# Layer 0's attention in a fused two-layer kernel: first routing in three bursts, first rows on ScalarE, later statistics and routing behind the attention

## The reference

```python
x = x + tanh(g_xattn[0]) * L0_xattn(layernorm(x), ctx, ctx)   # 16 heads of 8 channels, softmax
x = x + tanh(g_ffn[0])   * L0_ffn(layernorm(x))               # 8 experts, the best 2 per token
x = x + tanh(g_xattn[1]) * L1_xattn(layernorm(x), ctx, ctx)   # one head, causal
x = x + tanh(g_ffn[1])   * L1_ffn(layernorm(x))               # 8 experts, each takes its best 17 tokens
```

## Time and profile before

| what | value |
|---|---|
| median of three timed runs | 1021.94 us (1019.55 to 1022.29) |
| profiled execution, span from first to last instruction | 1023.1 us |
| TensorE busy | 910.3 us (89%) |
| VectorE busy | 599.0 us (59%) |
| ScalarE busy | 554.5 us (54%) |
| GpSimd busy | 647.5 us (63%) |
| mean granted TensorE clock | 0.971 of 2.4 GHz |

### The profile page before, as it was taken

The page is one execution under the profiler, slowest core; times in us unless marked ns, Lnnn a source line. Parts: engine busy times, 40 slices in busy tenths (PEclk is TensorE's granted clock), DMA queues, the critical chain, the costliest instruction groups (busy, mean ns, idle before and its releaser), DMA issues.

```text
span 1023.1 us, 24907 instructions
## 1 busy us (share of the span) xinstructions
PE 910.3 (89%) x8860; PEld 761.7 (74%) x8860; DVE 599.0 (59%) x1580; ACT 554.5 (54%) x1313; POOL 647.5 (63%) x807
## 2 busy tenths in 40 slices
PE   5998999888439999899999999968998999999992
PEld 3776777667328989799989988865776766778881
DVE  6887889999527463245625769984635324433320
ACT  2787877776224545344544766635555455444440
POOL 6353455468754777677427777721886658878885
PEclk9999999999859999999999999999999999999997
DMA  9364433112525656666566663141354635575453
GB/s 372 119 205 159 144 138 131 36 48 75 179 81 166 215 166 218 199 195 190 162 182 194 194 238 104 54 112 42 67 74 46 123 37 54 95 93 54 50 57 44
DMA packets 130154, 130.73 MB, mean 128 GB/s; under 512 B 32882, under 2 KB 102770, under 8 KB 129138
## 3 DMA queue, kind: packets, MB, share of 16 engines
q1 hardware_dynamic: 99810, 91.69, 28.5%
q0 software_dynamic: 28928, 29.91, 18.1%
q10 hardware_dynamic: 1296, 7.54, 1.8%
HBM read 53.88 MB, written 49.62 MB: 101 GB/s over the span
## 4 chain that ended last, share of the span: by engine, by line
PE 56%; DVE 11%; DMA 11%; issue 8%; POOL 8%; ACT 3%; SPq 1%; ACTq 0%; POOLq 0%; DVEq 0%
PE psum L875 9%; PE psum L891 9%; PE psum L1060 8%; PE psum L1050 8%; POOL xg L2062 5%; DMA xg<-work,place 4%; PE psum L681 3%; PE psum L1014 2%; DVE w_sb L1201 2%; PE psum L668 2%; PE psum L698 2%; DMA out_x<-ln_sb,dest 1%; DMA odd<-ln_sb,dest 1%; PE psum L865 1%; POOL odd L2154 1%
## 5 line engine op out<-in xcount | busy, mean ns | idle before, releaser
L1848 ACT ACTIVATE hid_sb<-psum,work 128x128 f32<-128x128 f32 (+1 forms) x424 | 145.8, 412 | 159.3 <-PE psum L875 156.8
L2076 POOL DMA_INDIRECT work<-yg,place x128 | 123.1, 962 | 63.5 <-issue 35.7
L875 PE MATMUL psum<-work 128*128 128x128 f32 (+1 forms) x848 | 151.8, 323 | 3.1 <-issue 2.9
L891 PE MATMUL psum<-w_sb,hid_sb 128*128 x1192 | 150.2, 275 | 0.0
L891 PEld LDWEIGHTS psum<-w_sb,hid_sb 128*128 128x128 f32 x1192 | 144.8, 192 | 2.1
L1050 PE MATMUL psum<-work,w_sb 128*128 128x272 f32 (+2 forms) x512 | 131.1, 397 | 5.1 <-ACT ctx_sb L1949 3.1
L875 PEld LDWEIGHTS psum<-work 128*128 128x128 f32 x848 | 125.3, 194 | 13.1 <-issue 5.6
L2154 POOL DMA_INDIRECT out_x<-ln_sb,dest x68 | 106.2, 1561 | 45.1 <-DVE ln_sb L1655 24.8
L2062 POOL DMA_INDIRECT xg<-work,place x104 | 101.5, 976 | 51.7 <-issue 25.3
L1949 ACT ACTIVATE ctx_sb<-psum,w_sb 128x272 f32<-128x272 f32 (+2 forms) x256 | 115.8, 488 | 26.3 <-PE psum L1050 22.6
L1060 PE MATMUL psum<-ctx_sb,w_sb 128*128 128x272 f32 (+2 forms) x512 | 128.1, 392 | 0.0
(11 more groups left out here) (264 smaller groups left out, 1614.1 us busy)
## 6 DMA issues: line engine op xcount, KB each, us to landing
work<-w_sb SPq DMA_DIRECT2D x76, 322.0 KB
work<-xg SPq DMA_DIRECT2D x73, 128.0 KB
yg<-yg_sb SPq DMA_DIRECT2D x73, 128.0 KB
xg<-yg_sb SPq DMA_DIRECT2D x24, 384.0 KB, 4.0
ctx_sb<-tok SPq DMA_DIRECT2D x8, 1088.0 KB, 6.4
ctxn<-sums_sb SPq DMA_DIRECT2D x64, 64.0 KB, 2.0
out_x<-x_sb SPq DMA_DIRECT2D x16, 256.0 KB, 2.0
odd<-yg_sb SPq DMA_DIRECT2D x10, 384.0 KB, 3.2
```

Of the source, the lines that this page charges most:

```text
L875: e.matmul(banks[UP_BANKS[c]][:, 0:cols], w1g(b)[:, c * P:c * P + P], xgT_sb[:, u % 2, at:at + cols], start=True, stop=True).then_inc(s_up, 1)
L891: ins = e.matmul(banks[DOWN_BANKS[b % 2]][:, n * D:n * D + D], hid0[:, b % 2, c, n * P:n * P + P], w2_sb[:, bass.ds(number, 1), c, :].rear ...
L1848: e.activation(hid0[:, b % 2, c, 0:cols], banks[UP_BANKS[c]][:, 0:cols], ACT.Gelu, bias=w1g(b)[:, HID + c:HID + c + 1]).then_inc(s_hg, 1)
L2076: e.indirect_dma_start(dst[:, k, :], None, yg_dram[h], at).then_inc(s_get[i], 16)
```

## The change

The first routing is drawn together: `FIRST_STEPS` runs four steps of part 0 in iteration 16, three in 17 and two in 18, counting is in iteration 17 (was 20) and owners in 19 (was 25). Puts begin in iteration 19 (was 25). Part 0's rows are made by ScalarE at the end of its iterations (`first_rows`), with the same eight buffers and waits; VectorE keeps the rows of parts 1 and 2. The router statistics of tiles 24 to 63 leave iterations 15 to 34 and are made in iterations 32, 33 and 34, 12, 12 and 16 tiles, ahead of `invert`; in iteration 34 the folding of layer 1's weights follows. GpSimd's moments for these tiles leave the loop and follow part 0's puts in three calls of 16, 8 and 16 tiles. Part 1's routing leaves the attention loop: it runs in blocks 1, 2, 5, 6 and 7, two steps in each, with its counting in block 4 (was iteration 34); part 2's starts in block 8 (was 5) and goes on in 9, 10, 11 and 14 to 19, its counting in block 13 (was 11), the softmax in 14 (was 12), the gates in 20 (was 18).

```diff
--- before.py
+++ after.py
@@ -83,11 +83,12 @@
 BS = UNIT // P
 
 LOGITS_IN = 15
-COUNT_IN = LOGITS_IN + 5
-
-
-PUT_FROM = 25
-PUT_BY = (2, 4, 5, 7, 10, 13, 15, 18, 21, PARTS[0][1])
+FIRST_STEPS = {LOGITS_IN + 1: 4, LOGITS_IN + 2: 3, LOGITS_IN + 3: 2}
+COUNT_IN, OWNERS_IN = LOGITS_IN + 2, LOGITS_IN + 4
+
+
+PUT_FROM = LOGITS_IN + 4
+PUT_BY = (1, 2, 4, 5, 6, 7, 9, 10, 12, 13, 15, 17, 19, 22, PARTS[0][1])
 
 
 def put_by(p):
@@ -106,9 +107,9 @@
 ROUTE1_FROM = 7
 
 
-ROUTE_IN = {NP - 1: 1, NP: 2, NP + 1: 1, NP + 2: 1}
-ROUTE_AT = {0: 1, 1: 1, 2: 1, 3: 1, 4: 1, 5: 1, 6: 1, 7: 1, 8: 1, 12: 1, 13: 1, 14: 1, 15: 1, 16: 1, 17: 1}
-COUNT_AT, SOFTMAX_AT, GATES_AT = 11, 12, 18
+LATE_STATS = {NP: (12, 18), NP + 1: (18, 24), NP + 2: (24, NP)}
+ROUTE_AT = {1: 2, 2: 2, 5: 2, 6: 2, 7: 2, 8: 1, 9: 1, 10: 1, 11: 1, 14: 1, 15: 1, 16: 1, 17: 1, 18: 1, 19: 1}
+COUNT_AT, SOFTMAX_AT, GATES_AT = {4: 1, 13: 2}, 14, 20
 
 
 SPREAD_AT = 11
@@ -846,8 +847,6 @@
                     turn_weights()
                 if p == COUNT_IN:
                     count0(0)
-                if p == NP + 2:
-                    count0(1)
                 if p % 2 == 0 and g < NG:
                     turn(g % 2, B_P, s_ln, s_lt, s_lnT, g)
                 if p % 4 == 1 and 0 <= (p - 5) // 4:
@@ -910,8 +909,8 @@
                 if b == 1:
                     multiply_bias()
                     output_bias(1, wo1_sb[:])
-                if b == COUNT_AT:
-                    count0(NPARTS - 1)
+                if b in COUNT_AT:
+                    count0(COUNT_AT[b])
                 if b > 0:
                     down0(b - 1, number)
 
@@ -1168,15 +1167,10 @@
 
             def put_rows(t):
                 w.wait_ge(s_momr, t // TS + 1)
-                if t < PARTS[0][1]:
-                    w.wait_ge(s_bias_row, 1)
-                    w.wait_ge(s_put[t % 4], 32 * (t // 4 - 1))
-                    dst = rows0(t)
-                else:
-                    at = t - PARTS[1][0]
-                    if at >= RING:
-                        w.wait_ge(s_put[t % 4], 32 * ((t - RING) // 4 + 1))
-                    dst = rows_sb[:, at % RING, :]
+                at = t - PARTS[1][0]
+                if at >= RING:
+                    w.wait_ge(s_put[t % 4], 32 * ((t - RING) // 4 + 1))
+                dst = rows_sb[:, at % RING, :]
                 e.tensor_scalar(dst, x_sb[:, t, :], rstd[:, t:t + 1], nmr[:, t:t + 1], ALU.mult, ALU.add).then_inc(s_rows, 1)
 
 
@@ -1386,21 +1380,19 @@
                 if 0 <= p - 3 < NP:
                     add_output(p - 3)
                 stats0(20 + 2 * p, 2)
-                if 0 <= p - 3 < NP:
+                if 0 <= p - 3 < PARTS[1][0] // 2:
                     stats_router(p - 3)
+                for late in range(*LATE_STATS.get(p, (0, 0))):
+                    stats_router(late)
                 if 0 <= p - 2 < NP:
                     invert(p - 2)
-                if LOGITS_IN < p < LOGITS_IN + 10:
+                for _ in range(FIRST_STEPS.get(p, 0)):
                     next(first_part)
-                if p == COUNT_IN + 5:
+                if p == OWNERS_IN:
                     for _ in owners0(0):
                         pass
                 if p == NP + 2:
                     fold_weights()
-                for _ in range(ROUTE_IN.get(p, 0)):
-                    next(side)
-                for t in range(rows_by(p - 1), rows_by(p)):
-                    put_rows(t)
 
 
             def copy_tokens(u):
@@ -1763,6 +1755,12 @@
                 if t == TG - 1:
                     ins.then_inc(s_ln, 1)
 
+            def first_rows(t):
+                w.wait_ge(s_momr, t // TS + 1)
+                w.wait_ge(s_bias_row, 1)
+                w.wait_ge(s_put[t % 4], 32 * (t // 4 - 1))
+                e.activation(rows0(t), x_sb[:, t, :], ACT.Identity, bias=nmr[:, t:t + 1], scale=rstd[:, t:t + 1]).then_inc(s_rows, 1)
+
             def turned_weights():
                 w.wait_ge(s_fm, 1)
                 e.copy(ln_sb[:, ROUTER, 0:3, :].rearrange("p n d -> p (n d)"), banks[0][:, 0:3 * P]).then_inc(s_wT, 1)
@@ -1824,8 +1822,6 @@
                     turned_weights()
                 if p == COUNT_IN:
                     copy_counts(0)
-                if p == NP + 2:
-                    copy_counts(1)
                 if p % 2 == 0 and g < NG:
                     w.wait_ge(s_q, g - 1)
                     copy_turned(g % 2, B_P, s_lt, s_lnT, g)
@@ -1837,6 +1833,8 @@
                     repeat_rden(p - 2)
                 if p // 2 + 2 < NG:
                     norm0(p // 2 + 2, (0, 1) if p % 2 == 0 else (2, 3))
+                for t in range(rows_by(p - 1), rows_by(p)):
+                    first_rows(t)
 
 
             def up0(b):
@@ -1862,8 +1860,8 @@
 
                 if b == SOFTMAX_AT:
                     exponentials0()
-                if b == COUNT_AT:
-                    copy_counts(NPARTS - 1)
+                if b in COUNT_AT:
+                    copy_counts(COUNT_AT[b])
 
                 if b in (NORM1_FROM, NORM1_FROM + 1):
                     norm1(b - NORM1_FROM, range(TG))
@@ -1992,8 +1990,8 @@
                 if raised:
                     step.done(ins)
                     ins = e.tensor_scalar(nmr[:, lo:lo + n], nmr[:, lo:lo + n], 1.0, None, ALU.add)
-                ins.then_inc(s_done, 1)
-                made[s_done.num] += 1
+                ins.then_inc(s_done, n // TS or 1)
+                made[s_done.num] += n // TS or 1
                 w.wait_ge(s_done, made[s_done.num])
 
             def moments_twice(router, first):
@@ -2094,15 +2092,16 @@
                     first, router = 2 * (p + 5), 2 * (p - 7)
                     if router < 0:
                         moments(first, TS, s_st0, first + TS, s_mom)
+                    elif router < PARTS[1][0]:
+                        moments_twice(router, first)
                     elif first < NT:
-                        moments_twice(router, first)
-                    else:
-                        moments(router, TS, s_st1, router + TS, s_momr)
+                        moments(first, TS, s_st0, first + TS, s_mom)
                 if p == LOGITS_IN:
                     add_logits(*PARTS[0])
                 for t in range(put_by(p - 1), put_by(p)):
                     put(t)
-            moments(NT - TS, TS, s_st1, NT, s_momr)
+            for lo, n in ((24, 2 * TS), (40, TS), (48, 2 * TS)):
+                moments(lo, n, s_st1, lo + n, s_momr)
             for t in range(PARTS[1][0], NT):
                 put(t)
             def moments1(lo):
```

## The result

The changed kernel takes 1037.12 us (median of four runs, 1033.30 to 1042.77); the kernel before, run beside it, 1020.75. The medians differ by 16.4 us; the ratio is given as 1.0142, 95% interval 1.0107 to 1.0176, which is slower by some 14.5 us. The sign was forecast, the size was not; 1037.1 lies outside the range of 1020 to 1032.5. The profiled execution is the fastest of the four (1033.30 us, span 1031.5), so the two traces differ by 8.4 us only, and what follows explains those. Lines such as L2060 are from here on those of the kernel that is spoken of; the changed kernel's lie some lines above those of the kernel before.

What follows compares the result with a forecast made beforehand. GpSimd's run of puts, begun when part 1's places are ready, was taken to set the time at block 41. Places 19.4 us later relative to block 0's start, which gains 14.5, gave +4.9: median 1026.8 us, range 1020 to 1032.5.

Steps and rivals of the forecast that it cites:

- What sets the end: At block 41 the end follows part 1's places through GpSimd's puts; VectorE waits some 20 us for the get.
- F: Start of the first expert block's (block 0's) matmuls: 299.78 us before, forecast 285.3, a gain of 14.5 us.
- Attention, iterations 16 to 19: VectorE's iterations with moved routing steps take 11.7, 12.4, 10.3 and 7.1 us; iteration 20 starts at 177.5.
- Iterations 20 to 31: Attention loop bound by TensorE at 7.0 us an iteration; last reduction at 255.0 us, 3.5 later than before.
- The 1 us for ScalarE's rows: Attention loop: ScalarE's 24 rows, 10.6 us over fourteen iterations, mostly fit and add 1 us, between 0 and 4.
- The drain: After the last reduction: last output 23.9 us later (28.35 before), then 3.3 us of statistics and 1.5 of folding.
- F to places: From block 0's first matmuls to part 1's places in block 7: 37.3 us, 19.4 later relative to that start.
- From the places to the landed get: GpSimd's run of puts and the first get, with their DMAs, keep their 111.9 us unchanged.
- Slower through ScalarE: Rival, 12%: ScalarE's rows delay TensorE in each attention iteration; last reduction near 262 us, end 1034.
- Even: Rival, 27%: same mechanism but smaller, with shorter routing runs, hidden statistics and no clock term: +1 us, 1019 to 1025.
- Faster: Rival, 12%: the drain is shorter, giving -2.4 us, or block 41 does not wait for the get, giving 1007.
- The clock: Attention loop: TensorE's waits in iterations 16 to 18 lower its granted clock, costing 0.5 us, between 0 and 3.

Runs made afterwards that it cites:

- e9: Kernel before with only early routing bursts, puts from iteration 19, part 0's rows by ScalarE, and three zero fills an iteration: 1012.16 us against 1023.51, ratio 0.9895.
- c0: The changed kernel run again, unaltered, on a slower chip where the kernel before takes 1257.54 us: ratio 1.0298 to the kernel before.
- e1: The changed kernel with three zero fills in each SyncE iteration instead of two, slower chip: ratio 1.0169 to the kernel before.
- e8: The changed kernel with part 0's rows made by VectorE again, slower chip: ratio 1.0290 to the kernel before.
- b0_before: The kernel before, unaltered, profiled on a slower chip for comparison: span 1258.9 us.
- e6_places_late: The kernel before with only part 1's last routing steps, and part 2's, four blocks later, slower chip: ratio 1.0125 to the kernel before.
- e2: The changed kernel with later parts' statistics, moments and routing put back as before, two fills an iteration, slower chip: ratio 1.0067 to the kernel before.
- e5: Kernel before with only early bursts, puts from iteration 19, ScalarE's rows and three fills an iteration, slower chip: ratio 1.0006.

## Why the prediction was right or wrong

**What sets the end: right on the faster kind.** "The end moves by as much as part 1's places move, not by as much as F moves." The first three lines of the table bear this out: from the kernel before to the changed one F comes 10.2 us earlier and the end 8.4 later, and in e9 part 1's first put moves 11.9 us forward and the span shrinks by 15.8. The idle stretch went where it was said, to VectorE's wait before the first combine. But that wait is 13.62 us and not some 20. VectorE reached the combine at 423.4 us, 133.7 after F, and not 128.8: part 0's blocks took longer. SyncE issues part 0's last results at 413.31 us, 123.7 after F; before it was 415.15, 115.4 after F. So even without the wait for the get, most of F's gain would have been gone by block 41.

**Attention, iterations 16 to 19: right, and the close hit is in part luck.** The reductions of 16 to 19 start at 134.01, 147.01, 158.92 and 169.30 us: 13.0, 11.9 and 10.4 apart where 11.7, 12.4 and 10.3 were summed; 17 waits 2.02 us for TensorE's denominators. Iteration 20 starts at 176.98, forecast 177.5. But from 16 to 20 it took 43.0 us and not 41.5, and the loop stood 1.9 us ahead before anything changed in it: the reduction of iteration 13 starts at 112.32 us, in the kernel before at 114.27. The two errors nearly cancel. In e9 this stretch takes 42.9 us too.

**Iterations 20 to 31: the step that failed.** "Eleven iterations at 7.0 give 252.2" left out the wait that GpSimd's put brings with it, and "Nothing in the change can fail to do what it says: the waits are explicit" passed over it. The last reduction is at 260.08, forecast 255.0. From iteration 20 to 31 it took 83.1 us where 77.5 were summed; e9, without the wait, takes 77.35. 5.5 us of the difference is the one stalled iteration; the others are 7.06 us in the mean. The condition was in the code (`put` waits for `s_fill`) and the price in reach: SyncE's fills are counted by its iterations, and the change moves the first put ahead of the last of them. The text had asked of GpSimd only how busy it is. On the slower kind of chip c0 against e1 shows by time that this wait costs; on the faster kind changed against e9 shows it by trace. The 1 us for ScalarE's rows and the 0.5 us for the clock can't be told apart in e9's sum; neither was much too low.

**The drain: right but for 0.8 us.** Last output 22.8 us after the last reduction (forecast 23.9), statistics of 3.18 us (forecast 3.3) and the folding behind it, all in VectorE's order of time:

```profile
282.89 0.48 DVE L1213 SCALAR_TENSOR_TENSOR x_sb<-psum,tg_sb,x_sb 128x256 f32<-128x256 f32 x1 [1.37 <-PE psum L720]
283.29 3.18 DVE L1185 BATCH_NORM_STATS2 stats<-x_sb 128x6 f32<-128x128 f32 x16
...
288.09 0.42 DVE L1403 COPY work<-psum 128x256 f32<-128x256 f32 x1
```

F is 289.63, forecast 285.3: 5.1 late by the reduction, 0.8 won back. But the forecast named VectorE alone; the chain shows that the last put (279.07) and its landing lead there too, at the same time. The puts were to "end near 272" and ended 8 us later, behind a loop that was 5.1 us late. And from the last put to F it took 10.6 us instead of 6.5: its landing took 5.90 us, before 2.23.

**F to places: right, 1.6 us short.** Cast at F + 38.7, done at 38.9, forecast 37.3. Two places were too low. `add_bias0(0)` came at F + 7.8 instead of 7.3. And block 1 cost more than its 2.3 us: the four steps held the copy of tokens, TensorE stood 1.96 us, and the next group ran at the lower level, 3.27 us for eight matmuls that take 1.73 otherwise. Chain of waits:

```profile
302.65 0.34 DVE work L1403
303.12 0.66 PE psum L864 x2
303.90 3.27 PE psum L874 x8
...
309.17 1.73 PE psum L874 x8
```

**From the places to the landed get: 3.5 us too long.** It was taken over as 111.9 us; from the first put to the combine it is 107.6 in the changed kernel and 108.0 in e9, against 111.1. The row of puts itself is as long as before (100.7 us from the first put's start to the last's, before 101.1). The last put's landing took 2.23 us and the get's 2.62, before 4.61 and 3.28; that makes 3.0 of the 3.5. I have no run that says why they landed sooner.

**The sum.** Forecast +4.9; last reduction +5.1 (the stall and what little else is in iterations 20 to 31 5.6, the bursts 1.4, less 1.9 for the earlier start); drain -0.8; places +1.6; the get -3.5; behind the combine +1.0. That makes 8.3, against 8.4 between the two traces. So the fills are the largest term that was missed, and several smaller ones nearly cancel.

**What it leaves open** is about as large again. The medians differ by 16.4 us. Without the 5.5 us of the stall the changed kernel would take some 1032 us, an estimate, still at the upper end of the range; so the stall alone does not explain the distance from 1026.8. In every run that lists both, the time is 1.8 us longer than the span; by that the profiled execution of the kernel before took 1024.9 us, above all four that were timed (1019.39 to 1022.29) and 4.2 above their median, while the changed kernel's is 3.8 below its own. The forecast, summed against that one span and lowered by 1.2 us, took over part of this error. The changed kernel's four timed executions have spans of 1031.5 to 1041.0 us at mean granted clocks of 0.960 to 0.970. Only the fastest has a trace, so no row shows where a slower one loses. The shifted stages add waits like the one before 303 us, each with matmuls at the lower level behind it, but that this is the spread is a guess.

**The rivals.** "Slower through ScalarE" gave 262 for the last reduction and came near to it by number (260.08), by another mechanism. Against it stands e9, where the same rows leave iterations 20 to 31 at 7.03 us in the mean, and on the slower kind e8. "Even" fell with the 5.5 us. "Faster" named the right hinge: in e9, where the places are not put off, the gain of F is kept.

**The clock** was put at 0.5 us for the bursts, against 3 by the rule that the prediction quotes. The granted clock did fall there: it is 0.86 from 147 to 159 us and 0.76 from 170 to 177, where the kernel before shows 1.00 from 136 to 166.6. What it cost can't be read apart from the bursts' 1.4 us. In the stalled iteration it is 0.87 over 8 us, and 0.50 in the 7 us before block 0. Behind TensorE's 1.96 us of idle time before 303.12 us it is 0.69 from 302 to 307.5, and the group of eight matmuls there takes 1.5 us longer than the next. As far as it goes, this agrees with the rule of the Trainium skill ("TensorE: Matmul & The Clock Gate", section "What's actually happening") that "activity releases the throttle", and at a shorter gap than the 3 us that I had thought of.

## What to carry to other kernels

Before an operation is moved forward on an in-order engine, list every semaphore it waits for and find when each producer finishes by its own schedule: a wait that has always been satisfied is invisible in the trace of before, and what it holds up is whatever is queued behind. Find the one run of work that has no slack (on the faster kind of chip GpSimd's 40 tiles of puts) and measure any plan by when that run starts: the first half of this change with three fills an iteration gains 1% there, and the fills' wait and the deferral of part 1's routing turned it into a loss. Ask again on another chip whether that run is still the one without slack. Work deferred from a busy stage is not free because a later stage looks idle: ask what the deferred result is the first input of.

## What the runs showed that I had not expected

The same kernel takes 1021 to 1024 us on some chips and 1255 to 1263 on others, steadily. ScalarE's groups from 300 us to the end on one of the latter (b0_before, columns: busy us, mean ns, idle before and what ended it):

```profile
L1848 ACT ACTIVATE hid_sb<-psum,work 128x128 f32<-128x128 f32 (+1 forms) x424 | 148.4, 411 | 346.5 <-remote 184.5 <-PE psum L875 149.7 <-issue 9.8
```

The activation itself takes the same time (411 ns); 184.5 us of idle time before it end on something the profile doesn't name. VectorE too stands for no semaphore of the kernel ahead of block 41 there (e6_places_late):

```profile
567.72 0.42 DVE L1430 TENSOR_TENSOR yg_sb<-psum,work 128x256 f32<-128x256 f32 x1 [22.88 <-issue]
568.06 0.73 DVE L1438 SCALAR_TENSOR_TENSOR x_sb<-work,gate,x_sb 128x128 f32<-128x128 f32 x2
```

So in these executions the combine follows 14.5 to 32 us after the get's issue and does not visibly wait for it. And the get does not wait for the puts either. In b0_before the last put is issued at 480.84 us, and GpSimd then stands 48.5 us before the first get. The profile names no releaser, but `get` waits for two things, all puts and part 0's last results, and these SyncE issues 3.0 us before (SyncE's and GpSimd's order of time):

```profile
527.32 0.50 SPq L550 DMA_DIRECT2D yg<-yg_sb  x1
530.32 0.99 POOL L2076 DMA_INDIRECT work<-yg,place  x1 [48.53 <-issue]
```

In all fifteen traces of this kind the get follows part 0's last results by 3.0 to 3.3 us, 40 us or more behind the last put; on the faster kind it follows them by 9.8 us (before), 19.7 (changed) and 6.7 (e9), and the last put by 5.4, 3.0 and 3.7. So on the slower kind the run of puts has slack, and the pace of part 0's blocks sets the get. That pace depends on where the later routing stands: from the first matmul of block 0 to part 0's last results it takes 199 to 203 us in the three kernels that route part 1 as before (b0, e2, e5), and 215 to 226 in the twelve that defer it. From the get to the end it is 723 to 733 us in all of them, while the get itself moves by 44. Deferred routing costs on both kinds, then, but not by the same path: here through the blocks that now hold it, there through the places and the run of puts. Which of its steps slow the blocks, no experiment has separated.

The difference matters for a verdict too: the first half with three fills gains 1.05% on one kind of chip and nothing (1.0006) on the other, while every version with late places that was timed loses: the changed kernel on both, the others on the slower kind.
